# P·V products of an attention kernel placed one key tile per step instead of two per two steps

## What is computed

```python
xn = layernorm(x)
# attention, 16 heads of 32, causal, with ALiBi bias
q, k, v = proj(Wq, bq), proj(Wk, bk), proj(Wv, bv)
scores = where(causal, -inf, q @ k.T / sqrt(32)) - slope[h] * |i - j|
out = softmax(scores) @ v
attn = out @ Wo.T + bo
# mixture of experts: 8 experts of inner width 352, top 2 by softmax gate
gate_up = xn @ w1.T;  g, u = split(gate_up)
ffn = sum over the two chosen experts of weight * ((silu(g) * u) @ w2.T)
result = x + attn + ffn
```

## Time and profile before

| | |
|---|---|
| median of 3 runs | 1571.19 us (1569.72 to 1571.23) |
| the profiled execution's own time | 1569.72 us |
| its span, first to last instruction | 1567.9 us |
| PE busy over the span | 1430.5 us, 91% |
| DVE, ACT, POOL busy | 1039.1, 890.5, 565.0 us |
| weight loads of line 1177 | 3328 |

### The profile page before, as it was taken

One profiled execution on the slowest core, in us unless ns is written; L12 is line 12 of the kernel. 1 busy time (PEld: TensorE's weight loads), 2 busy tenths in 40 slices (PEclk: granted clock), 3 DMA queues, 4 the chain that ended last, 5 costly groups with the idle time before them and its releaser, 6 DMA issues.

```text
span 1567.9 us, 35531 instructions
## 1 busy us (share of the span) xinstructions
PE 1430.5 (91%) x12763; PEld 919.9 (59%) x12763; DVE 1039.1 (66%) x2501; ACT 890.5 (57%) x2019; POOL 565.0 (36%) x595
## 2 busy tenths in 40 slices
PE   4898989998997999989899898999889999999995
PEld 2566655665665666666566466665456666656562
DVE  7887887766878868777788977788333333333331
ACT  5677777665767767776776555788222222222221
POOL 5111132121123212113312233232137777777775
PEclk9999999999999999999899999999999999999998
DMA  7345231433423254443214232144968888888784
GB/s 265 106 135 136 86 108 59 124 102 110 134 75 99 83 161 142 135 140 93 89 48 139 81 104 76 57 148 150 357 129 138 134 131 137 138 135 134 129 135 47
DMA packets 171350, 193.28 MB, mean 123 GB/s; under 512 B 87536, under 2 KB 121072, under 8 KB 171056
## 3 DMA queue, kind: packets, MB, share of 16 engines
q1 hardware_dynamic: 143760, 151.67, 35.4%
q0 software_dynamic: 26128, 37.24, 14.1%
q10 hardware_dynamic: 1296, 2.11, 0.4%
HBM read 93.45 MB, written 53.74 MB: 94 GB/s over the span
## 4 chain that ended last, share of the span: by engine, by line
PE 64%; DVE 13%; issue 7%; SPq 5%; ACT 4%; DMA 4%; POOL 2%; DVEq 0%; ACTq 0%; POOLq 0%
PE S L1238 16%; PE O L1177 7%; DVE arena L1542 5%; PE T L1161 5%; PE S L1150 4%; PE T L1118 4%; PE M L1269 4%; PE O L1269 4%; SPq L993 4%; PE M L1118 2%; PE M L1161 2%; PE S L1118 2%; PE S L1161 2%; PE T L1200 2%; DMA out<-arena 2%
## 5 line engine op out<-in xcount | busy, mean ns | idle before, releaser
L1739 ACT ACTIVATE arena<-arena,mneg 128x1024 f32<-128x1024 f32 (+7 forms) x512 | 395.5, 773 | 86.6 <-DVE mneg L1542 84.1
L1542 DVE CUSTOM_DVE_ANT_0 arena<-S,cF,nsl 128x1024 f32<-128x1024 f32 (+7 forms) x512 | 411.4, 811 | 35.2 <-PE S L1150 23.7
L1238 PE MATMUL S<-arena 128*128 x1704 | 268.1, 314 | 6.3 <-issue 6.2
L1895 POOL DMA_INDIRECT out<-arena x142 | 222.2, 1565 | 105.6 <-ACT arena L1802 57.9
L1150 PE MATMUL S<-arena 96*128 96x512 f16 (+3 forms) x768 | 215.2, 335 | 23.9 <-DVE mneg L1542 22.2
L1238 PEld LDWEIGHTS S<-arena 128*128 128x128 f16 x1704 | 167.2, 98 | 104.3 <-issue 7.1
L1161 PE MATMUL T<-cF,arena 128*128 128x128 f32 x1198 | 203.1, 281 | 25.0 <-DVE arena L1558 18.8
L1177 PE MATMUL O<-arena 128*32 128x128 f32 (+1 forms) x3328 | 179.1, 331 | 10.9 <-DVE arena L1578 10.5
L1161 PEld LDWEIGHTS T<-cF,arena 128*128 128x128 f32 x1198 | 144.2, 144 | 67.4 <-issue 21.2
L1756 ACT ACTIVATE arena<-T 128x128 f32<-128x128 f32 (+3 forms) x275 | 126.8, 466 | 94.3 <-PE T L1161 93.3
L1672 DVE COPY arena<-T 128x512 f16<-128x512 f16 x71 | 30.2, 425 | 220.2 <-PE T L1253 217.2
(11 more groups left out here) (209 smaller groups left out, 2349.4 us busy)
## 6 DMA issues: line engine op xcount, KB each, us to landing
arena<-arena SPq DMA_DIRECT2D x192, 128.0 KB, 2.4
arena<-in_w1T SPq DMA_DIRECT2D x64, 352.0 KB, 3.4
arena<-in_x SPq DMA_DIRECT2D x64, 256.0 KB, 3.5
w_d<-arena SPq DMA_DIRECT2D x32, 352.0 KB, 2.9
arena<-w_d SPq DMA_DIRECT2D x16, 704.0 KB, 6.2
arena<-in_w2T SPq DMA_DIRECT2D x32, 256.0 KB, 2.9
out<-arena SPq DMA_DIRECT2D x32, 256.0 KB, 3.0
xn_d<-arena SPq DMA_DIRECT2D x24, 256.0 KB, 2.1
```

The source lines that it names most:

```text
L1238: tp = pe.matmul(y[:, i * 512:i * 512 + I], xT[:, s % XDEEP, 4 * a + c, :], weights[:, bass.ds(reg[s] + (w_ * NX * W1N + c * 2 * I + i * I ...
L1542: dve.tensor_tensor_reduce(ring[r][:, 0:w], SBK[o.bank["score", u]][:, 0:w], rel[:, S - w:S], nsl[:, hh:hh + 1], 3.0e38, ALU.add, ALU.min, ...
L1739: act.activation(ring[r][:, 0:w], ring[r][:, 0:w], ACT.Exp, bias=mneg[:, m:m + 1], scale=-1.0, accum_out=rs[:, k, c:c + 1]).then_inc(sems[ ...
L1895: pool.indirect_dma_start(out=halves, out_offset=bass.IndirectOffsetOnAxis(row[:, part, s:s + 1].bitcast(U32), 0), in_=yo[:, s % YDEEP, c0 ...
```

## The change

The first item of a group is placed in the unit in which the generator is made, not one unit later. After that one item is placed in each unit, where two were placed in every second unit. Of a group with eight items the last two (6 and 7) stay together. The step `rt` follows the last item, as before.

| items | before: units after the generator is made | after |
|---|---|---|
| 8 | 0,1 at +1; 2,3 at +3; 4,5 at +5; 6,7 and `rt` at +7 | 0 to 5 at +0 to +5; 6, 7 and `rt` at +6 |
| 7 | the same, 6 alone with `rt` at +7 | 0 to 5 at +0 to +5; 6 and `rt` at +6 |
| 6 | 0,1 at +1; 2,3 at +3; 4,5 and `rt` at +5 | 0 to 4 at +0 to +4; 5 and `rt` at +5 |
| 5 | 0,1 at +1; 2,3 at +3; 4 and `rt` at +5 | 0 to 3 at +0 to +3; 4 and `rt` at +4 |

```diff
     def values(u):
-
         n = len(pv_work(unit(u)[2]))
-        yield
         o.take("O", "pv", u)
         for i in range(n):
-            if i and i % 2 == 0:
-                for _ in range(2):
-                    yield
             add("pv", u, i, inc=i == n - 1)
+            if i < 6 and i + 1 < n:
+                yield
         o.count["pv", u] = o.count["pv", u, n - 1]
         add("rt", u)
         tpv[u] = True
```

## The result

The changed kernel takes 1588.88 us (median of 4 runs, 1588.02 to 1596.11) against 1571.21 us (4 runs, 1569.72 to 1572.89): ratio 1.0137, 95% interval 1.0105 to 1.017, or +17.7 us. On a second chip it took 1594.18 us against 1571.90, ratio 1.0152 (1.0126 to 1.0177). The forecast was 1602 us with a range of 1583 to 1622 and "slower" at 0.88. So the side is right, and the size is a bit over half of the forecast 31 us (seven tenths on the second chip). Thirteen executions of the changed kernel are on record with these, from 1584.39 to 1598.59 us, and their median is 1593.44 us: that puts the loss nearer to 22 us than to 17.7. The profiled execution is the one of 1593.44 us, span 1591.6, which is 23.7 us above the profiled execution before.

What follows compares the result with a forecast made beforehand. PE was taken to set the pace, busy 91% of the span, with some slack on DVE and ACT. Terms 46 - 14 - 3 + 2 + 0 = 31 us on the median 1571.2 gave 1602 us, range 1583 to 1622.

Steps and rivals of the forecast that it cites:

- The number of runs and their price: P·V on PE: 400 runs instead of 224, 176 more at 0.26 us each, 46 us.
- What covers it: Added PE pauses fall into PE's waits for DVE or ACT: half of the coverable 28 us, minus 14 us.
- fewer, by some 15 us: Sign of being right: PE's waits of scores and transposes (lines 1150 and 1161) fall by some 15 us.
- issue: Sign of being right: P·V weight loads' idle time put down to no semaphore rises near 40 us above 50.6.
- The clock: Lower granted clock over the attention, 4% of 1020 us, 41 us; used in rivals, no term in the sum.
- If a quarter of that came back: Rival: nearly all pauses covered and a quarter of the lost clock returned, 18 - 10 = 8 us, 1579; chance 0.12.
- The shift within a pair: Items move from odd to even units: load per pair unchanged but for pauses, transposes' waits for copies 3 us less.
- New waits: Item 0 on PE waits for the transposes' copy, now nearer: bounds nothing or 19 us, 2 us taken.
- The bank `O`: First P·V item's wait for this PSUM bank keeps its two units of distance, as `rt` moves along.
- The end: Last group's output projection waits about 0.9 us less for POOL, against two more runs, 0.5 us: net 0.
- Faster: Rival: even spread of P·V feeds DVE and ACT better, waits and clock give back 55 us, 1562 us; chance 0.07.

Runs made afterwards that it cites:

- singles_late: The changed kernel's one item a unit, but started one unit after the generator is made, as in the kernel before; 1574.90 us, ratio 1.0012 to the kernel before.
- the light pair: The changed kernel and singles_late, each with less DVE and ACT work (256 columns for big units); 1549.57 and 1538.61 us, against 1521.33 for the kernel before so cut.
- after_again: The changed kernel unaltered, timed once more with the last group of versions on a second chip; 1594.18 us, ratio 1.0152 to the kernel before.
- pairs_early: The kernel before with its pairs of items kept but placed one unit earlier, 224 runs; 1572.22 us, ratio 1.0005 to the kernel before.
- rt_as_before: The changed kernel with the step `rt` kept in its old unit; 1634.08 us, ratio 1.0390 to the kernel before.
- runs_of_four: The kernel before with items 0 to 3 together at +1 and the rest together at +5, 128 runs; 1603.74 us, ratio 1.0201.

## Why the prediction was right or wrong

**The number of runs and their price** stood. 224 and 400 runs are in the traces. 46 us were forecast, from 0.26 us a run. The changed kernel's two profiles give 40 and 42, singles_late 44, the light pair 38 and 39: 0.22 to 0.25 us a run, at the lower end of the rows' 0.23 to 0.28 or just under it. The 0.26 taken was some 6 us too much in all.

**What covers it** stood in size for the waits: 14 us were taken, and they fell by 11 (first profile) and 14.5 us (second). The signs written down held too: the waits of scores and transposes "fewer, by some 15 us" (20.7 + 39.7 to 10.3 + 32.5, 17.6 us), and "issue" well above 50.6 us (104.7, 54 more, where 40 were named).

**The clock** was the term left out. It was used in a rival only ("If a quarter of that came back") and stood at zero in the sum. In the two profiles 10.4 and 11.4 us of 38.0 came back; by all executions it is less, 5 us in the changed kernel (46 to 41) and 2 in after_again (47 to 45). Over the eleven versions with full work the clock's part in all executions rises with the waits of the profile, from 33 us at 55.7 us of waits to 63 at 116.0: a fitted line gives about 0.5 us of clock for 1 us of waits, an estimate from the table. The windows show the same in one kernel: the clock is at 1.00 in the full one, at 0.83 and 0.91 in the two with waits. A cover of 14 us in waits would so have come with some 7 us of clock.

**The sum again, with what the first profile shows:** pauses 40 where 46 stood, waits and clock together 21 given back where 14 + 3 stood for the waits alone, behind the last P·V 5 us more where "Net 0" and 2 us of new waits stood: 40 - 21 + 5 = 24 us, the distance of the two profiled executions. Price and cover were both off toward a larger loss, the end toward a smaller one. The mechanism stood, and the sum was 7 us high against the profile, 9 against after_again's median and 13 against the median of the result.

**The shift within a pair** was forecast at -3 us of waits for copies. The rows of line 1161 that were quoted (30.5 us) stand at 27.7 in the changed kernel, so this holds, but the waits for the row minimum gave back 10 us. They were not named there. pairs_early, where they fall by 9 us with the runs unchanged, shows that the earlier place is enough for it.

**New waits:** 2 us were taken for item 0 and the copies; one such wait of 0.8 us is in the trace. The bank `O`, said to keep its distance, went from 10.5 to 13.9 us. rt_as_before shows what lay behind that sentence: one unit less costs 40 to 45 us.

**The end** failed. "Net 0", and "SP's and POOL's queues are passed by nothing but the step `scaled`". The output projection's stores and reloads follow the scaling, and they hold POOL: 4.4 us there, and some 3 us more at the start of the expert part, where PE waits for the weights.

**The rivals.** "Faster" rested on the even spread, and was turned down since "the items per pair of units stay as they are". The spread is real, in singles_late it repays all of 44 us. In the changed kernel waits and clock repaid a bit over half (21 to 26 of 40 to 42 us). Why the early singles get less back than the late ones (42 us) is not fully settled. Some 4 us of it are the wait for POOL, and some 3 are the longer wait for the bank `O` (14.7 against 11.2 us, the early items' wait for copies included); the 3 us at the start of the expert part come on top. The rest may lie in the items of an eight-item group in the even units, which already carry most transposes, but no run here tests that alone.

## What to carry to other kernels

Count how often a stream of matmuls changes the array's shape, not only how many matmuls it has: read the price from the starts around the change, and test it with one tiny matmul put in between. But how finely the work is spread decides about as much: pauses fall into waits, and waits carry some of the clock with them, so put a clock term into the sum wherever the windows show it under 1, and read it from all executions: here the profiles of the changed kernel showed two to five times as much come back. Before calling a step's shift free, follow every step that is timed by it, down to the store and the reload in another engine's queue. The best of the sizes tried here lay between, three items a run, 7 us under the kernel before.

## What was not expected of the hardware

A tiny matmul of 8 columns cost 0.25 us between two matmuls of the narrow shape and nothing that could be measured where the shape changed anyway (160 of them: +20.9 and -1.7 us). And the clock moved with the waits, about half as much over all versions: with 24.8 us less of waits in singles_late it took 13 to 14 us less by all executions, with 35.5 us more in runs_of_four 17 to 18 us more.
